# Second normalisation and row selection moved from programs of their own into the cross attention's program

## The reference, cut to what matters

```
x = layernorm(x + gated_delta_attention(x))            # first stage, untouched
x = layernorm(x + cross_attention(x, mask, ctx))       # 32 heads of 16, self and context part, projection Wo
x = layernorm(x + ffn(x))
ffn(h):
    scores = einsum("btd,d->bt", h, w_router)          # one score a row, per batch of 256 rows
    idx = sort(top_k(scores, 32))                      # 32 of 256 rows of each of the 8 batches
    sel = h[b, idx]                                    # 256 rows in all
    ... rms norm, q/k/v with bias, rotary by idx, causal attention over the 256 rows, gated MLP ...
    h[b, idx] = gate * processed + (1 - gate) * sel    # gate = sigmoid(score)
```

## Time and profile before

| | |
|---|---|
| median of 3 runs | 3035.65 us (3032.44 to 3039.57) |
| the profiled execution | 3029.36 us, its span 3027.6 us |
| PE, DVE, ACT busy over the span | 92%, 58%, 45% |
| cross attention | from 1679 us to 2725.4 us |
| from its last instruction to the first projection of the last stage | 87.0 us |

### The profile page before, as it was taken

The page is one execution under the profiler, slowest core; times in us unless marked ns, Lnnn a source line. Parts: engine busy times, 40 slices in busy tenths (PEclk is TensorE's granted clock), DMA queues, the critical chain, the costliest instruction groups (busy, mean ns, idle before and its releaser), DMA issues. The chain is left out here.

```text
span 3027.6 us, 81744 instructions
## 1 busy us (share of the span) xinstructions
PE 2799.4 (92%) x34610; PEld 1757.1 (58%) x34610; DVE 1742.4 (58%) x4879; ACT 1361.6 (45%) x3288; POOL 503.3 (17%) x626
## 2 busy tenths in 40 slices
PE   7999999999999999999997799999999999871999
PEld 3555555555555555555655566666666666550466
DVE  5565656565556555555564266666665666667533
ACT  3343434343434343434332266666666666660131
POOL 1212121212121212121211210210102101000030
PEclk9999999999999999999997899999999999995999
DMA  5010101101101011011001000000000000003051
GB/s 186 13 44 19 38 18 30 33 13 30 44 19 40 16 30 33 13 30 44 19 23 47 22 1 12 8 5 12 2 12 5 8 12 1 2 2 152 7 216 63
DMA packets 92842, 100.10 MB, mean 33 GB/s; under 512 B 38080, under 2 KB 84416, under 8 KB 91200
## 3 DMA queue, kind: packets, MB, share of 16 engines
q1 hardware_dynamic: 92320, 94.35, 9.7%
q0 software_dynamic: 160, 0.52, 0.0%
HBM read 90.01 MB, written 4.85 MB: 31 GB/s over the span
## 5 line engine op out<-in xcount | busy, mean ns | idle before, releaser
L209 PE MATMUL dr_p<-x_t,dr_w_g 128*128 128x512 f32 x1536 | 740.1, 609 | 10.9 <-DMA dr_w_g<-in_w_in 7.5
L1301 ACT ACTIVATE xa_probs<-xa_probs,xa_low 128x256 f32<-128x256 f32 x1024 | 437.0, 497 | 44.8 <-DVE xa_low L1379 43.3
L209 PEld LDWEIGHTS dr_p<-x_t,dr_w_g 128*128 128x128 f32 x1536 | 268.1, 191 | 227.0 <-issue 216.8
L1379 DVE CUSTOM_DVE_ANT_0 xa_probs<-xa_s,xa_mask 128x256 f32<-128x256 f32 x512 | 213.7, 417 | 286.3 <-PE xa_s L1219 286.3
L645 DVE SCALAR_TENSOR_TENSOR dr_acc<-dr_p,dr_taps,dr_acc 128x510 f32<-128x510 f32 (+2 forms) x384 | 285.0, 742 | 23.9 <-ACT dr_acc L501 15.9
L1232 PEld LDWEIGHTS xa_t<-ident,xa_probs 128*128 128x128 f32 x2048 | 222.0, 141 | 125.1 <-issue 67.0
L1232 PE MATMUL xa_t<-ident,xa_probs 128*128 128x128 f32 x2048 | 283.7, 279 | 4.4 <-ACT xa_probs_t L1307 4.4
L1307 ACT ACTIVATE xa_probs_t<-xa_t 128x512 f32<-128x512 f32 x256 | 152.7, 597 | 263.7 <-PE xa_t L1232 261.5
L1379 DVE CUSTOM_DVE_ANT_0 xa_probs<-xa_s,xa_zeros 128x256 f32<-128x256 f32 x512 | 214.3, 419 | 0.0
L1388 DVE COPY xa_probs_t<-xa_t 128x512 f32<-128x512 f32 x256 | 176.3, 689 | 60.7 <-PE xa_t L1232 47.1
L1247 PE MATMUL xa_o<-xa_probs_t,xa_val 128*32 128x128 f32 x4096 | 139.2, 276 | 48.8 <-DVE xa_probs_t L1388 28.9
(11 more groups left out here) (317 smaller groups left out, 4769.9 us busy)
## 6 DMA issues: line engine op xcount, KB each, us to landing
dr_alpha<-alpha_rows SPq DMA_DIRECT2D x64, 254.0 KB, 4.2
dr_w_g<-in_w_in SPq DMA_DIRECT2D x48, 256.0 KB, 6.0
dr_alpha<-alpha_rows SPq DMA_DIRECT2D x32, 256.0 KB, 5.5
x_t<-in_x_t SPq DMA_DIRECT2D x4, 1024.0 KB, 7.1
tokens<-in_x_tok SPq DMA_DIRECT2D x1, 4096.0 KB, 16.0
dr_wo_g<-in_w_out SPq DMA_DIRECT2D x8, 512.0 KB, 3.9
xa_ctx_b<-in_ctx_t SPq DMA_DIRECT2D x8, 512.0 KB, 3.8
ff_tall<-in_fw_o SPq DMA_DIRECT2D x1, 4096.0 KB, 12.2
```

Source lines behind the costliest of these rows:

```text
L209: mm = pe.matmul(bank[:, :], w_g[:, k, m, :], x_t[:, k, 2 * S * batch:2 * S * (batch + 1)], start=(k == 0), stop=(k == KC - 1))
L1301: op = act.activation(at, at, ACT.Exp, bias=low[:, v % 3, i, kind:kind + 1], scale=-1.0)
L1379: op = dve.tensor_tensor_reduce(out=probs[:, v % 3, i, kind, :], in0=bank_s[i][:, kind * S:(kind + 1) * S], in1=mask[:, par, q, :] if kind ...
```

## The change

The second layer norm, the scores and the choice of rows are no longer done for all rows after the cross attention, but batch by batch in its program, one batch late. The three blocks in between are gone.

- d4 and d14: after each `out`, DVE also takes `bn_stats` and `bn_aggr` of the tile.
- end of d5: ACT takes the root (`root`) of the batch before.
- end of d6: DVE does `rate`: reciprocal, normalisation of two tiles, two scores, the diagonal.
- d15: PE spreads the scores of the batch before over the partitions (256 columns), ACT copies them.
- start of d0, a batch later: DVE does `choose` (own scores, ranks, chosen).
- d3: PE counts the seats, DVE makes `pick`. This use is early, so the projection q1 of d3 moves from inner to outer.
- What is left for the last two batches stands in `TAIL`.
- The loads of w_router, before and counts are issued after the first batch's ctx and mask, and DVE waits for them at its start. The other loads of the last stage are issued at the start of `ffn_phase`, `wide` in eight parts with a semaphore each, the bias after the first.
- The gather is now the start of `ffn_phase`; `place` and `places` are made after the first rms norm. `doubled` and `gate` share memory with `x_mid` and `by_sin`.

```diff
@@ cross_phase: order
             if d == 1:
                 return ("turn", QT * b - 1) if b else None
+            if d == 15:
+                return ("spread", b - 1) if b else None
+            if d == 3:
+                return ("count", b - 2) if b > 1 else None
             return (EARLY[d], b + 1) if d in EARLY and b + 1 < B else None
...
-        TAIL = [("norm", LAST // 2 - 1), ("turn", QT * B - 1), ("out", QT * B - 1)]
+        TAIL = [("norm", LAST // 2 - 1), ("turn", QT * B - 1), ("out", QT * B - 1), ("count", B - 2), ("spread", B - 1),
+                ("count", B - 1)]
@@ pe_make
+            elif what == "spread":
+                wait(pe, diag_made, at + 1)
+                mm = pe.matmul(bank[:, 0:S], all_ones[:, :], diag[:].rearrange("p c n -> p (c n)"), start=True, stop=True)
+            elif what == "count":
+                wait(pe, chosen_made, at + 1)
+                pe.matmul(bank[:, 0:NC], counts[:, SEL:SEL + P], chosen[:, at, :], start=True, stop=False)
+                mm = pe.matmul(bank[:, 0:NC], all_ones[:, :], chosen_before[:, at, :], start=False, stop=True)
@@ ACT
+            elif what == "spread":
+                wait(act, ranked, NC * at)
+                op = act.activation(score_rows[:, :], bank[:, 0:S], ACT.Copy)
...
+        def root(act, b):
+            wait(act, averaged, QT * (b + 1))
+            act.activation(ln_den[:, b, :], moments[:, b, :, 1], ACT.Sqrt, bias=ln_eps[:, 0:1]).then_inc(ln_rooted, 1)
...
                 if late(u):
                     act_take(act, late(u))
+                if u % HALVES == 5 and u > HALVES:
+                    root(act, u // HALVES - 1)
                 if u % 2:
@@ DVE
                 v.tensor_tensor(tokens[:, at, :], tokens[:, at, :], bank[:, :], ALU.add).then_inc(taken_dve, 1)
+                wait_taken(v, use)
+                v.bn_stats(stats[:, at, :], tokens[:, at, :]).then_inc(added, 1)
+                wait(v, added, at + 1)
+                v.bn_aggr(moments[:, at // QT, at % QT, :], stats[:, at, :]).then_inc(averaged, 1)
+
+        def rate(v, b):
+            wait(v, ln_rooted, b + 1)
+            v.reciprocal(ln_den[:, b, :], ln_den[:, b, :]).then_inc(ln_inverted, 1)
+            wait(v, ln_inverted, b + 1)
+            for c in range(NC):
+                at = tokens[:, NC * b + c, :]
+                v.tensor_scalar(at, at, moments[:, b, c, 0:1], ln_den[:, b, c:c + 1], ALU.subtract, ALU.mult).then_inc(row_normed, 1)
+            for c in range(NC):
+                wait(v, row_normed, NC * b + c + 1)
+                op = v.tensor_tensor_reduce(out=weighted[:, c, :], in0=tokens[:, NC * b + c, :], in1=w_router[:, :], ...,
+                                            accum_out=score[:, b, c:c + 1])
+            op.then_inc(row_scored, 1)
+            wait(v, row_scored, b + 1)
+            if b:
+                wait(v, made, made_at["spread", b - 1])
+            v.tensor_tensor(diag[:], ident[:, None, :].to_broadcast([P, NC, P]), score[:, b, :, None].to_broadcast([P, NC, P]), ALU.mult)\
+                .then_inc(diag_made, 1)
+
+        def choose(v, b):
+            wait_taken(v, ("spread", b))
+            # 2 tensor_tensor_reduce of 128 columns (own score), wait,
+            # 2 scalar_tensor_tensor of 256 (equal), wait, 2 of 256 with a sum (greater), wait, 2 tensor_scalar (chosen)
...
             for u in range(LAST):
+                if u % HALVES == 0 and u > HALVES:
+                    choose(dve, u // HALVES - 2)
                 if u + 1 < LAST:
                     tops(u + 1, 0)
...
                 if late(u):
                     dve_take(dve, late(u))
+                if u % HALVES == 6 and u > HALVES:
+                    rate(dve, u // HALVES - 1)
+            choose(dve, B - 2)
             for use in TAIL:
                 dve_take(dve, use)
+                if use[0] == "out":
+                    rate(dve, B - 1)
+                if use[0] == "spread":
+                    choose(dve, B - 1)
@@ ffn_phase
+                for to, source in ((table, tables_dram), (ln, ln_dram), (causal, causal_dram)):
+                    sp.dma_start(to[:], source).then_inc(small_loaded, 16)
+                for m in range(8):
+                    sp.dma_start(wide[:, :, m * D:(m + 1) * D], w_qkv_dram[:, :, m * D:(m + 1) * D]).then_inc(qkv_loaded[m], 16)
+                    if m == 0:
+                        sp.dma_start(bias, bias_dram.partition_broadcast(P)).then_inc(bias_loaded, 16)
...
-                pe.wait_ge(qkv_loaded, 16)
                 for n, (m, r) in enumerate(STEPS):
                     wait(pe, biased, n - 1)
+                    if r == 0:
+                        pe.wait_ge(qkv_loaded[m], 16)
```

More of the change, by code:

```diff
@@ L972, in delta_phase @@
         a.clear()
[L975 to L1036, removed]
-                    sp.wait_ge(stored, 16 * NT)
@@ L1041 @@
+SEL = S // 8
+ROWS = B * SEL
+RT = ROWS // P
+BT = B // RT
+FH, FKV, FD = 16, 8, 128
+FI = 2048
+FF_EPS = 1e-6
+LOWEST = -3.4028234663852886e38
 XH, XD = 32, 16
@@ L1364, in dve_take @@
                                 parts[:, 0], parts[:, 1], ALU.add).then_inc(normed, 1)
+            elif what == "count":
+                wait(v, made, made_at[use])
+                v.tensor_copy(seat[:, at, :], bank[:, 0:NC]).then_inc(taken_dve, 1)
+                wait_taken(v, use)
+                for c in range(NC):
+                    op = v.scalar_tensor_tensor(out=pick[:, c, at, :], in0=counts[:, 0:SEL], scalar=seat[:, at, c:c + 1],
+                                                in1=chosen[:, at, c:c + 1].to_broadcast([P, SEL]), op0=ALU.is_equal, op1=ALU.mult)
+                op.then_inc(picked, 1)
             else:
@@ L1613, in ffn_phase @@
[L1613 to L1614 removed]
+def ffn_phase(nc, tokens, chosen_rows, tables_dram, causal_dram, ln_dram, bias_dram, w_qkv_dram, w_o_dram, w_gu_dram, w_down_dram,
+              ident, out):
+    pick, labels, counts = chosen_rows
     with ExitStack() as stack:
@@ L1623, in ffn_phase @@
         angles = a.sb("angles", [P, RT, P])
+        table = a.sb("table", [P, NC, P])
+        place = a.sb("place", [P, RT])
         row_scores = a.sb("row_scores", [P, RT])
@@ L1662, in ffn_phase @@
         junk = by_sin
+        gate = by_sin[:, :, 0:ROWS]
         low = f.sb("low", [P, 4, RT])
@@ L1831, in root @@
                     act.activation(den[:, n, r:r + 1], sumsq[:, n, r:r + 1], ACT.Sqrt, scale=1.0 / D, bias=eps[:, 0:1]).then_inc(rooted, 1)
+                for r in range(RT):
+                    act.wait_ge(gathered, 3 * BT * r + BT)
+                    act.activation(rows[:, r, :], banks_of_row[r][0][:, :], ACT.Copy).then_inc(gathered_copied, 1)
+                    act.wait_ge(gathered, 3 * BT * (r + 1))
+                    act.activation(angles[:, r, :], banks_of_row[r][1][:, 0:P], ACT.Copy).then_inc(gathered_copied, 1)
+                    act.activation(row_scores[:, r:r + 1], banks_of_row[r][2][:, 0:1], ACT.Copy).then_inc(gathered_copied, 1)
                 act.wait_ge(eps_made, 1)
                 for r in range(RT):
+                    act.wait_ge(gathered_copied, 3 * r + 1)
                     root(0, r, rows)
```

242 lines of the change are left out of this document (89 added, 153 removed).

## The result

The changed kernel takes 2991.18 us, the median of 4 runs (2984.0 to 2991.59), beside 3035.64 us for the kernel before on the same chip: ratio 0.9847, 95% interval 0.9829 to 0.9866. The forecast was 2992, in a range of 2979 to 3010.

What follows compares the result with a forecast made beforehand. PE was busy 92% of the span, but an 87.0 us bridge after the cross attention hung on a DVE chain. 3029.36 - 59.2 (bridge) + 15.5 (cross attention) = 2985.7, plus 6.3 to the median: 2992 us, range 2979 to 3010.

Steps and rivals of the forecast that it cites:

- The bridge: Cross attention's last add to the last stage's first projection: 27.75 us instead of 87.0, 59.2 gained (bounds 55 and 62).
- The change of program: In the bridge, with 36 semaphores cleared instead of 21: 2.7 us for 1.91 (1.9 if none were clearing, 3.3 if all).
- Gather to first projection: End of the bridge: 13.2 us for 15.08, from 2.39 less, 1.0 more waiting for small loads, 0.5 less by the clock.
- The wide weights: Load for the last stage's projections: stays hidden, first part landing 7.1 us after issue with 4.7 to spare.
- Rival 4: Last stage: first part of `wide` or the bias is late, about +4 us, 2996; chance 0.03.
- Cross attention, batches 1 to 6: Units lengthened past their idle time: 1.5 us lost in batch 1, 9.5 in batches 2 to 6.
- Last batch: Batch 7 of the cross attention: 1.1 (d0), 0.5 (d3), 1.4 (d5) and 1.5 (d6), together 4.5 us lost.
- rival 5: Partly exposed chain: ACT's second load, `rate`, clock falling in last batch; 20 to 35 us more, 3010 to 3029; chance 0.06.
- The sum: Whole kernel: 3029.36 - 59.2 + 15.5 = 2985.7 us for an execution like the profiled one, 6.3 more for the median.
- Rival 2: ACT's table switches: each costs a 1.38 us drain beside the load, nine times, 12.4 us, giving 3004; chance 0.08.
- Rivals 1 and 3: Cross attention: Rival 1 says no slack; the other says it hides all the added work, 2973 to 2982 us, chance 0.08.
- Rival 1: Cross attention: no slack in the handover, all added work shows, about 11 us a batch, 77 in all, 3053; chance 0.03.

Runs made afterwards that it cites:

- e1: Changed kernel with the wide weights in one transfer with one semaphore, bias behind them: 3002.2 us, ratio 0.9882 to the kernel before.
- e3: Changed kernel with VectorE's `choose` at the end of d2, not the start of d0: 2985.2 us, ratio 0.9825 to the kernel before.
- e4: Changed kernel with PE's seat count in d15, not d3, and a q projection back in d3: 2996.78 us, ratio 0.9862 to the kernel before.
- e8: Kernel before with only its wide weights cut in eight parts, bias after the first: 3053.67 us, ratio 1.0057 to the kernel before.
- e2: Changed kernel with ScalarE's root replaced by a plain copy of the variance: 2979.97 us, ratio 0.9817 to the kernel before.

## Why the prediction was right, point by point

**The bridge: right, 61.1 gained for a forecast of 59.2.** By its terms, measured from end to end: stats 0.98 (0.9); root 0.33 (1.7); `rate` 2.88 (3.0); seats, spread and copy 1.77 (1.95); `choose` 2.67 (2.6); seats and `pick` 1.76 (1.7). Together 10.4 for 11.85, and nearly all of the difference is one term, the root. Its table load is not in the chain at all:

```profile
2736.59 1.28 ACT L1275 ACT_TABLE_LOAD   x1
2742.10 0.30 ACT L1275 ACTIVATE xa_ln_den<-xa_moments,xa_ln_eps 128x2 f32<-128x2 f32 x1 [4.22 <-DVE xa_moments L1365]
```

ACT loads the table as soon as it gets to the root in its own order, and waits for the moments after that. I had put the load behind the wait.

**The change of program: 3.2 us for 2.7, inside its bounds of 1.9 to 3.3.** The bounds were made for "all of it clearing" and "none of it", and the measured value lies at the first. The experiment agrees: without the block of clearing it is 0.5.

**Gather to first projection: 12.2 for 13.2.** The wait for the small loads is 0.16 for 1.0, since the causal mask lands 2.9 after its issue. The clock's part, of which I took 0.5, is visible too: the first four transposes take 0.66 us and not 1.12.

**The wide weights: covered, as said, with the reason shown.** No projection waits, and the first bias add of DVE comes when the bias has just landed. Rival 4 didn't occur. What the prediction hadn't seen is SP's issue, 21.5 us for seven parts. It is harmless here, and it put 20 us on the path when the kernel before was given the same parts. I had costed it at nothing without naming what stood behind SP.

**Cross attention, batches 1 to 6: 8.7 us for 11.0.** The places were right and the sizes a little high: d0 0.91 for 1.1, d3 and d4 -0.78 for -0.7, d6 1.33 for 1.4 and 0.1, all of it root and loads and none of it `rate`. Nothing showed at d4, d14 or d15, as said. The experiments undid each of these alone and each gave back its own figure.

**Last batch: 7.9 us for 4.5, the step that was mis-sized.** The steps cost 3.9 (94.00 - 90.11): `choose` 0.91 for 1.1, seats 0.30 for 0.5, root 1.25 for 1.4, `rate` with ACT's second load 1.15 for 1.5, and 0.30 in d12 that no term had. The rest is TensorE's clock. 5.3 us of the changed kernel's last batch went there and 1.3 (91.40 - 90.11) of the last batch before. I had the clock only in rival 5, as part of a loss of 20 to 35 us, so a part of that rival's mechanism did occur.

**The sum.** For an execution like the profiled one I had 2985.7 and it took 2984.0. The errors were -1.9 in the bridge, +1.0 in the cross attention (-2.3 and +3.4, with rounding) and -0.8 in the stages ahead of it, which the change doesn't touch. That they nearly cancel is luck. Their sizes add to 8.4, and had all gone one way the time would still have been inside the range. The 6.3 from the profiled execution to the median had no mechanism behind it either. Here the profiled execution is 7.2 below its median, but in e1, e3, e4 and e8 it is the slowest of its kernel. So that the median came out at 2991 for 2992 is in this part luck too.

**Rival 2 is dead.** The cross attention has seven pairs of loads, and in all seven no load stands more than 0.02 us from its neighbours. The Trainium skill, "ScalarE: Activation LUTs", section "What ACT_TABLE_LOAD costs", gives every switch a drain of some 1.38 us beside the load; the trace agrees with its 1.28 for the load and doesn't show the drain, and the measurement decides. Rivals 1 and 3 fail on the batch: 1.48 us, neither 11 nor 0. Rival 1's terms add up to 11.9 and not to 11, so it stood for some 3060; that changes nothing here.

**What stays open.** In the last batch d12 is 0.30 longer (7.08 for 6.78 at full clock) in the kernels with the moved steps, and no step of the change stands there. The one exception is e4, with the count in d15 and not in d3: its d12 is 6.78. In the others DVE stands still for 0.21 us in d12 with nothing in the trace that it waits for, and in e4 it doesn't; what ties that to the place of the count isn't shown. Why the clock falls in other units from one execution to the next is not settled either.

## What to carry to other kernels

The average slack of an engine says only that moved work may be free; where in its order it is put decides. The same root and loads cost 1.33 us a batch ahead of a copy that PE waits for, and nothing behind it, and 2.6 us of `choose` cost 0.91 at d0 and nothing at d2. That holds where projections fill PE; in the last batch, which has none, the better places still cost 1.40 and 0.92. So list the unit lengths before and after, and move each step that shows.

When a stage is shortened, ask which loads lay under it. And when a transfer is cut in parts, ask what stands behind the queue that issues them: here that was a whole block in one kernel and nothing in the other.

Where PE has only short work left, at the last turn of a loop, a few matmuls that nobody reads can cost less than the clock they keep up gives back: 94.00 for 99.27 us in the last batch here.

## What the runs showed of the hardware that was not expected

- SP can be held by a row of large transfers: 2.8 us for each further part of 1 MB (seven in 19.56 us, behind a first part and the bias), while each of the small loads took 0.33 to 0.51 us in the changed kernel. Size alone doesn't do it: the one transfer of 8 MB was issued in 0.43 us in the kernel before (at 2730.04), and at its start three of 1 MB took 1.90 together (at 6.97). What does isn't settled by any run.
- ACT's table load goes ahead of the wait of the activation that needs it (2736.59, with the root at 2742.10), and a later root of another block finds that table loaded (e2, where it was not, loads at 2755.73).
- The block that clears the 36 semaphores of the cross attention takes about 2.7 us of the 3.2 between two programs.
- The clock differs from one execution of a kernel to the next, in the last batch (99.27 and 97.81 us for the same 14 units) and in batches 3 and 4 (127.93 and 127.94 us in one, 129.07 and 129.22 in the other). The last out step is at either level too. DVE waits 5.26 us for it in four of eleven profiles without the extra matmuls (the two shown of before and after are among them) and 8.1 to 8.2 in the other seven; with them it was 5.26 in both. The four are each the fastest execution of their kernel, and four of the seven are the slowest of theirs. This is the right size for a part of the 6 to 7 us by which the profiled executions stood below their medians, but that link is argued, not shown.
